# New places for every step of a 16-sequence, four-part pipeline, and output loads issued ahead of reciprocal loads

## What is computed

```python
x = L0_attn_a_x                                  # (16, 512, 256)
x = x + attn_a(_layernorm(x), Wq, bq, Wk, bk, Wv, bv, Wo, bo)
x = x + ffn(_layernorm(x), w_gate, w_up, w_down)
x = x + attn_b(_layernorm(x), Wqkv, Wout, bout)
x = x + ffn(_layernorm(x), w_gate, w_up, w_down)
# attn_a: 16 heads of 16; key allowed if |i-j| <= 32 or i < 4 or j < 4; softmax; output projection
# attn_b: num = exp(q_rot.k_rot / 4) with rotary q, k; den = sum over all keys of exp(q.k / 4)
#         attn = where(causal, num / den, 0); output projection
# ffn:    h = silu(x wg^T) * (x wu^T); h wd^T, int32 weights scaled by 1/127, hidden size 768
```

## Time and profile before

| | |
|---|---|
| three runs, median (lowest to highest) | 2423.99 us (2398.24 to 2429.8) |
| the profiled execution | 2416.59 us, span 2414.7 us |
| busy: PE, ACT, DVE, POOL | 1964.4, 1442.0, 1438.2, 789.2 us |
| TensorE clock granted, mean | 0.904 |
| chain that ended last: PE, DVE, DMA, ACT, SP's queue | 45%, 16%, 14%, 13%, 7% |
| transfers: packets, moved | 129635, 201.86 MB |

### The profile page before, as it was taken

How to read it: one execution, slowest core, us unless ns; L and a number is a source line. 1 busy time by engine, 2 the same in 40 slices (tenths; PEclk the granted TensorE clock), 3 DMA queues, 4 the chain that set the end, 5 groups by cost and what they waited for, 6 DMA issues and landing times.

```text
span 2414.7 us, 63331 instructions
## 1 busy us (share of the span) xinstructions
PE 1964.4 (81%) x25221; PEld 1424.3 (59%) x25221; DVE 1438.2 (60%) x2971; ACT 1442.0 (60%) x3580; POOL 789.2 (33%) x1131
## 2 busy tenths in 40 slices
PE   2667788978898998889788898978889897987775
PEld 2455466656575665657566665756666565655544
DVE  3364556757575675767575575757566576745533
ACT  1215566676756667675666666565666767567480
POOL 0013243333333333333334333332433334333331
PEclk7778899989898899999899898989899899988887
DMA  5222425142433414243342414333251424332320
GB/s 154 53 61 61 94 69 119 52 101 64 116 70 90 109 58 112 55 107 82 95 91 77 102 54 102 78 101 85 78 120 53 98 66 116 73 90 68 80 57 32
DMA packets 129635, 201.86 MB, mean 84 GB/s; under 512 B 26768, under 2 KB 60560, under 8 KB 129312
## 3 DMA queue, kind: packets, MB, share of 16 engines
q1 hardware_dynamic: 129344, 197.80, 33.5%
HBM read 67.87 MB, written 51.52 MB: 49 GB/s over the span
## 4 chain that ended last, share of the span: by engine, by line
PE 45%; DVE 16%; DMA 14%; ACT 13%; SPq 7%; issue 4%; POOL 1%; POOLq 0%; DVEq 0%; ACTq 0%
PE gu_bank L1035 12%; DMA xn<-o_scr_A 7%; PE gu_bank L1063 6%; PE gu_bank L999 6%; ACT s_bank L1149 5%; PE d_bank L1051 5%; SPq L566 4%; DMA xn<-o_scr_B 4%; ACT probs_B L1139 3%; PE s_bank L930 3%; DVE top L1296 3%; PE s_bank L966 2%; DMA o_scr_B<-o_raw 2%; PE gu_bank L1009 2%; PE s_bank L799 2%
## 5 line engine op out<-in xcount | busy, mean ns | idle before, releaser
L1149 ACT ACTIVATE s_bank<-s_bank 128x512 f32<-128x512 f32 x1024 | 601.3, 589 | 307.1 <-PE s_bank L930 306.3
L1539 POOL TENSOR_TENSOR h<-tmp,h 128x512 fp32r<-128x512 f32 x192 | 247.1, 1287 | 418.8 <-DVE h L1421 418.5
L1139 ACT ACTIVATE probs_B<-s_bank 128x512 f32<-128x512 f32 x640 | 331.4, 615 | 39.0 <-PE s_bank L951 37.1
L1556 POOL TENSOR_SCALAR_AFFINE_SELECT probs_B<-probs_B 128x256 f32<-128x256 f32 x512 | 202.7, 420 | 383.6 <-ACT probs_B L1139 383.2
L930 PE MATMUL s_bank<-pack_b 48*128 48x512 f16 x1024 | 179.9, 402 | 163.8 <-DVE o_raw L1327 83.5
L1035 PE MATMUL gu_bank<-xT,w_g 128*128 128x256 f32 x1536 | 233.9, 296 | 15.5 <-DVE xT L1397 7.8
L1035 PE MATMUL gu_bank<-xT,w_u 128*128 128x256 f32 x1536 | 225.2, 290 | 2.6 <-DVE src_a L1433 2.1
L1035 PEld LDWEIGHTS gu_bank<-xT,w_g 128*128 128x128 f32 x1536 | 202.9, 195 | 40.9 <-DVE tmp L1404 16.3
L1051 PE MATMUL d_bank<-w_d,h 128*128 128x256 f32 x1536 | 224.8, 290 | 2.1 <-POOL h L1539 2.1
L1051 PEld LDWEIGHTS d_bank<-w_d,h 128*128 128x128 f32 x1536 | 195.4, 190 | 31.4 <-issue 25.1
L1035 PEld LDWEIGHTS gu_bank<-xT,w_u 128*128 128x128 f32 x1536 | 201.1, 193 | 20.1 <-DVE src_a L1433 7.8
(11 more groups left out here) (140 smaller groups left out, 3445.9 us busy)
## 6 DMA issues: line engine op xcount, KB each, us to landing
pack_b<-src_b SPq DMA_DIRECT2D x768, 64.0 KB, 2.4
pack_a<-src_a SPq DMA_DIRECT2D x384, 64.0 KB, 2.8
x<-in_L_attn_a_x_dram SPq DMA_DIRECT2D x32, 512.0 KB, 4.9
o_scr_A<-o_raw SPq DMA_DIRECT2D x64, 256.0 KB, 3.1
o_scr_B<-o_raw SPq DMA_DIRECT2D x64, 256.0 KB, 2.8
rden_on<-r_scr_A SPq DMA_DIRECT2D x32, 256.0 KB
xn<-o_scr_A SPq DMA_DIRECT2D x32, 256.0 KB
x_scr<-x SPq DMA_DIRECT2D x16, 512.0 KB, 2.7
```

What stands on the lines that cost most here:

```text
L1139: act.activation(probs["B"][:, i, :], score_bank("NP", n // 2, q, n % 2)[:, :], ACT.Exp, scale=SM_SCALE)\
L1149: act.activation(bank[:, :], bank[:, :], ACT.Exp, scale=SM_SCALE, accum_out=den[:, 0, j, 2 * tile + e, t:t + 1]).then_inc(den_exp, 1)
L1539: pool.tensor_tensor(h[1][:, i % 2, :], tmp[:, i % 2, :], h[0][:, i % 2, :].bitcast(F32), ALU.subtract)\
L1556: ins = pool.affine_select(a, a, [[0, 2], [1, P]], ALU.is_ge, 0.0, base=0, channel_multiplier=-1)
```

## The change

Every place in `AT` is set anew. The length of a turn stays at 425, and `START` holds the same `425 * q` for all blocks, so it changes nothing by itself. In `places()`, in the waits and in the arithmetic nothing is changed. Each engine issues the same instructions as before, in another order, and ring banks and `o_raw` buffers follow the order. All entries of the table differ; a few lines:

```diff
+START = {block: tuple(TURN * q for q in range(SEQS))
+         for block in ("A", "PA", "VA", "NA", "OA", "F1", "PB", "VB", "RB", "B", "OB", "F2")}
...
-    "OAOR": (694,),
-    "OAOL": (705,),
+    "OAOR": (792,),
+    "OAOL": (771,),
...
 def start_of(q, block):
-    return TURN * q
+    return START[block][q]
```

More of the change, by code:

```diff
@@ L107 @@
-    "PBT": (899, 905, 913, 915),
-    "PBT1": (904, 906, 914, 916),
-    "PBT2": (911, 912, 919, 922),
-    "OAOR": (694,),
-    "OAOL": (705,),
[L112 to L184, removed]
[35 rows of a table added]
+    "VBC": (1046, 1074),
+    "VA": (334, 356),
+    "VAC": (376, 390),
+    "GW": (391,),
+    "GL": (419,),
+    "SL": (372, 381, 388, 389),
+    "GB": (365,),
+    "W": (1009, 1020, 1031, 1037),
+    "W1": (1014, 1021, 1032, 1038),
+    "W2": (1024, 1030, 1042, 1053),
+    "PAT": (315, 326, 327, 328),
+    "PAT1": (331, 336, 337, 338),
+    "PAT2": (358, 361, 362, 364),
+    "PBT": (999, 1002, 1003, 1006),
+    "PBT1": (1000, 1004, 1005, 1007),
@@ new lines @@
+    "PBT2": (1008, 1011, 1012, 1013),
+    "OAOR": (792,),
+    "OAOL": (771,),
+    "OAOM": (793, 795),
+    "OAOH": (811, 817),
+    "OAOW": (812, 818),
+    "OAO": (819, 822),
+    "OAOX": (826, 834),
+    "OBOR": (1450,),
+    "OBOL": (1480,),
+    "OBOM": (1481, 1483),
+    "OBOH": (1482, 1484),
+    "OBOW": (1488, 1489),
+    "OBO": (1490, 1494),
+    "OBOX": (1503, 1504),
+    "F2L0": (1510,),
+    "F2L1": (1511,),
+    "F2L2": (1517,),
+    "F2L3": (1518,),
+    "F2L4": (1519,),
+    "F2L5": (1520,),
@@ new lines @@
+    "F1L0": (835,),
+    "F1L1": (836,),
+    "F1L2": (842,),
+    "F1L3": (845,),
+    "F1L4": (846,),
+    "F1L5": (847,),
+    "PBL0": (965,),
+    "PBL1": (978,),
+    "PBL2": (985,),
+    "PBL3": (986,),
+    "PBL4": (987,),
+    "PBL5": (988,),
+    "NAL0": (254,),
+    "NAL1": (256,),
+    "NAL2": (292,),
+    "NAL3": (293,),
+    "NAL4": (294,),
+    "NAL5": (295,),
+    "PAX": (297,),
+    "PAXH": (312,),
+    "PAX1": (344,),
+    "F2X": (1521,),
+    "F2XH": (1522,),
+    "F2X1": (1558,),
@@ new lines @@
+    "F1X": (854,),
+    "F1XH": (864,),
+    "F1X1": (865,),
+    "PBX": (993,),
+    "PBXH": (994,),
+    "PBX1": (995,),
+    "F1G": (869, 887, 888, 905, 914, 941),
+    "F1GT": (873, 889, 904, 919, 927, 942),
+    "F1U": (870, 892, 903, 908, 931, 948),
+    "F1H": (876, 895, 906, 924, 934, 953),
+    "F1I": (878, 907, 922, 932, 947, 958),
+    "F1J": (884, 911, 923, 933, 952, 959),
+    "F1JL": (885, 912, 925, 935, 954, 960),
+    "F1FD": (891, 913, 926, 944, 955, 961),
+    "F1E": (938, 964),
@@ new lines @@
+    "F2G": (1533, 1542, 1548, 1593, 1608, 1623),
+    "F2GT": (1536, 1545, 1555, 1607, 1618, 1638),
+    "F2U": (1534, 1561, 1582, 1600, 1627, 1630),
+    "F2H": (1565, 1574, 1575, 1634, 1650, 1652),
+    "F2I": (1566, 1580, 1622, 1635, 1654, 1658),
+    "F2J": (1571, 1589, 1624, 1641, 1655, 1709),
+    "F2JL": (1577, 1597, 1625, 1644, 1660, 1710),
+    "F2FD": (1578, 1605, 1626, 1689, 1716, 1730),
+    "F2E": (1653, 1731),
+    "XL": (735,),
+    "BI": (736,),
+    "XS": (1780,),
+    "XA": (248,),
@@ L185 @@
+    "XO": (1001,),
+    "BP": (989,),
+    "XB": (1415,),
 }
```

## The result

The changed kernel takes 2313.3 us (median of 4 runs, 2308.38 to 2316.62) against 2423.4 (2398.24 to 2429.8), a ratio of 0.956 (0.949 to 0.963). The prediction said 2363, with 2320 as its low end. The direction was right, the size was not: about twice what I had summed. The profiled execution took 2316.6 us, 100.0 less than before's.

A forecast was written before the change was run, and what follows sets the result against it. It took the kernel to be bound, twice a turn, by a loop through HBM: store, load, scale, project. Terms summed to -3.8 us a turn, times 14 -53 us, from 2416.6 to 2363 us; range 2320 to 2425.

The forecast's parts named there:

- times 14: Whole run: the sum of -3.8 us per turn multiplied by 14, as waits occur 14 or 15 times; -53 us.
- OA's load goes early: -2.8: At OA: the earlier load of A's outputs removes OM's wait; 2.8 us less per turn, bounds 0 and 9.6.
- the PE work between T2 and O stays: At OA: PE's work ahead of O taken as unchanged, so the gain is much nearer 2.8 than 9.6 us.
- F1's layer norm no longer meets POOL: -1.2: Behind OA: L5 no longer runs beside POOL's JL 4; 1.2 us less per turn, bounds 0 and 1.2.
- PB's layer norm: +0.7: At PB: four exponentials now ahead of AH 0 on ACT, AT 0 ahead of L2; 0.7 us more per turn.
- The rest: +0.5: Other moves (F2's X1, CM 11 to 14, BT 0), each hidden but for a little; 0.5 us more per turn.
- OB's split: -1.5: At OB: AT 2 leaves the place ahead of OW (0.6), OW is faster clear of POOL (0.9); 1.5 us less per turn.
- +0.5 for DP 5: At OB: DP 5 now comes behind O's first half on PE; charged 0.5 us per turn, half of 1.03.
- OB's wait itself stays: 0: At OB: store-to-load chain unchanged on SP, so the wait of about 6.8 us and the low clock after it stay.
- the clock comes back: Rival, behind OB: a shorter wait removes the low clock; 4 us times 14 beyond the sum, 2310 us; chance 0.12.
- The slower rival, RL 1 late: RL 1, moved behind AD, comes late for PE's NP 5; 34 us slower in all, 2450 us; chance 0.08.

The follow-up runs named there:

- ol_early: Kernel before with one step moved, on SP alone: the load of A's outputs right behind the store of A's reciprocals; 2357.0 us, ratio 0.979.
- oa_part: Kernel before with all engines' and SP's 136 steps around OA, from before PA's T to F1's layer norm, in the changed order; 2339.1 us, ratio 0.972.
- mid_part: Kernel before with all engines' and SP's 152 steps from F1's layer norm to DT in the changed order, nothing else; 2439.0 us, ratio 1.011.
- ob_part: Kernel before with all engines' and SP's 102 steps around OB, from DT to F2's L1, in the changed order; 2402.2 us, ratio 0.9995.

## Why the prediction was too slow

The profiled execution came 47 us under the forecast: 21 us ahead of the first turn, where the sum had no term, and some 26 us in the turns, 78.9 instead of 53. Three steps failed: the product with 14, which left out the first turns; the choice of 2.8 within its bounds for OA's load, where the work ahead of O was taken as unchanged; and the sign of the last two terms.

- **"times 14"** failed first. I took the whole list's mean, 44.5 / 16 = 2.8, for a steady turn, and never looked at the first turns. There the wait was 7.3 us a case, and later 2.1. The first reciprocal came 21.0 us earlier, 14.3 of it by the early load alone, and my sum per turn had no place for that.
- **"OA's load goes early: -2.8"**: OM's wait is gone, as predicted, and the load alone gave 2.1 to 2.95 a turn. What failed is the reason for stopping there, that "the PE work between T2 and O stays". It didn't. BV 1 with its 32 matmuls and six matmuls of scores went from ahead of O to behind it. One turn of each kernel from PA's first T to A's first O, before and after (length, busy PE, PEld, DVE, ACT, POOL, granted clock):

```profile
1221.30:1247.98 26.68, 24.19 (x199) 17.66 (x199) 16.72 (x29) 15.03 (x40) 10.19 (x13) 1.00 0.52 111
```

```profile
1171.10:1193.66 22.56, 20.91 (x163) 16.60 (x161) 15.96 (x25) 14.59 (x39) 8.71 (x12) 1.00 0.42 93
```

Means over the ten or eleven turns of each trace between 450 and 1950 us, in brackets PE's idle time in them:

| us from one first matmul to the next | before | ol_early | oa_part | changed |
|---|---|---|---|---|
| PA's T to A's O | 27.1 (2.8) | 25.1 (0.9) | 22.6 (1.6) | 22.6 (1.7) |
| A's O to PB's T | 52.8 (5.3) | 52.3 (5.1) | 53.0 (4.1) | 52.7 (2.4) |
| PB's T to B's O | 28.7 (6.4) | 28.1 (6.4) | 28.1 (6.5) | 27.4 (7.1) |
| B's O to PA's T | 30.3 (4.5) | 29.7 (4.6) | 31.5 (5.0) | 30.5 (3.6) |

Of the 5.4 us of a full turn, 4.5 lie between PA's T and A's O: 2.0 came with the load, the rest with the order around OA. The work that left went into time in which PE was idle behind O, so the changed kernel needs no longer for that stretch than before. In oa_part's trace part of this is lost again behind OB: its full turns, 135.2 us, are as long as ol_early's, while the medians put it 18 us ahead.

- **"F1's layer norm no longer meets POOL: -1.2"**: L5 did come down from 2.62 us to 1.38. It did so with the stretch from F1 to DT (1.38 in mid_part, still 2.65 in oa_part), and it won nothing by itself, since L5 starts 1.1 us later behind O than before. In the turns shown PE's X begins 11.6 us behind O in both kernels. Before, then after:

```profile
1247.98 1.69 PE L999 MATMUL gu_bank<-wa_o,xT 128*128 128x256 f32 x12
...
1259.56 1.11 PE L1009 MATMUL gu_bank<-eye,xn 128*128 128x128 f32 x8
```

```profile
1193.66 1.68 PE L1002 MATMUL gu_bank<-wa_o,xT 128*128 128x256 f32 x12
...
1204.32 1.38 DVE L1393 TENSOR_SCALAR xn<-x,mv,root 128x256 f32<-128x256 f32 x4
...
1205.26 1.09 PE L1012 MATMUL gu_bank<-eye,xn 128*128 128x128 f32 x8
```

OM itself now loses 1.5 us to POOL.

- **"PB's layer norm: +0.7"** and **"The rest: +0.5"**, together +1.2, had the wrong sign. Most of these moves lie from F1 to DT and in the 35 untested steps, and with OA's and OB's stretches in place these together give 28 to 41 us. Some 17 to 20 us of it are the shorter and more even run from A2 to DT, which I had not looked for. Why the stretch costs 31 us when it is moved alone, and which steps make up for that, stays open.
- **"OB's split: -1.5"**, with +0.5 for DP 5: 0 to 1.3 a turn in the three comparisons. OW's time came down as predicted, but POOL's pass fell on OH, one instruction ahead.
- **"OB's wait itself stays: 0"** held for DVE (76.6 us) and nearly for PE. Its wait of 5.3 to 6.8 us in the full turns is split in two: DP 4 no longer waits for an AT behind OM, so PE stops for UL 0's copies, mostly 1.5 to 2.0 us, and then at O, 3.2 to 4.1.
- Of the **rivals**, "the clock comes back" (2310) is closest to the time. That its number fits is luck, since its 4 us a turn were to come behind OB, but part of it may be right. The mean clock rose from 0.904 to 0.927, though the stretch behind OB is no shorter. Among the 13 full turns of the kernel before, those with the higher clock are the shorter ones: 133.9 us at 0.97, 143.2 at 0.89. A straight line through them gives 136.6 at 0.956, the changed kernel's mean over its own. So my estimate from these rows is that 2 of the 5.4 us a turn go with the clock. That is a bound and no cause: in ob_part the clock rose and the time stayed. The slower rival, RL 1 late, didn't show: PE's waits for pack_b are UL 0's.

Where a term's size looks right it is in part luck: the 1.2 us of the layer norm were not won on the path, while the order around OA gave more than any term had for it.

## What to carry to other kernels

Read a wait case by case before multiplying its mean: in a pipelined kernel the first turns have nothing to cover it, and a sum per turn leaves them out. An instruction moves as a set with every load that it needs: OM moved ahead of one of its two loads cost some 34 us here, and the other load put back under an early OM cost 210. When a big reordering is taken apart by stretches, check that they add up to the whole: here 35 of 425 steps were in none of them, and a third of the gain can't be placed for that reason. And where a load waits for the last of several stores, split it: the part that was stored early can be loaded and worked on under the wait, which gave 74 us here.

## What the runs showed that I had not expected

In three turns of the kernel before, PE stops inside one group of 64 matmuls (L917, AV 0) for 2.28, 1.83 and 1.82 us, where nothing that the profile shows is waited for:

```profile
1153.49 0.85 PE L917 MATMUL s_bank<-probs_A,v_aug_A 64*17 64x96 f32 x43
1156.62 0.61 PE L917 MATMUL s_bank<-probs_A,v_aug_A 64*17 64x128 f32 x21 [2.28 <-issue]
```

From the first scores of A's global queries and keys to DT, the fourth, the seventh and the fourteenth turn take 15.2 to 15.9 us, the others 11.7 to 12.1. In all ten traces with the old order from F1 to DT these three are longer than the usual 11.7 us, 12.5 to 15.9; in some of these traces a few other turns are long as well, up to 14.1. In the ten with the new order every turn takes 11.4 to 11.7. That it depends on where instructions lie in the program is a guess; no run tested it.
